# Cross-attention in steps of two batches instead of one, with tails of the context turned on the chip and the last keys loaded once

## The reference, cut to what matters

```python
def cross_attn(x, context, Wq, Wk, Wv):      # x [16,64,512], context [16,1601,512], float32
    Q = x @ Wq
    K, V = (context @ Wk, context @ Wv)
    energy = jnp.einsum('bqd,bkd->bqk', Q, K)
    lengths = jnp.sum(energy[:, 0] != 0, axis=-1)      # counted, then used as a mask
    pad = jnp.arange(Sk)[None, None, :] >= lengths[:, None, None]
    energy = jnp.where(pad, NEG_INF, energy)
    score = jax.nn.softmax(energy / np.sqrt(DK), axis=-1)
    return jnp.einsum('bqk,bkd->bqd', score, V)
```

## Time and profile before

| | us |
|---|---|
| median of 3 runs | 998.28 |
| lowest and highest | 998.18, 999.06 |
| profiled execution | 997.61 |
| its span | 995.7 |

### The profile page before, as it was taken

How to read it: one execution, slowest core, us unless ns; L and a number is a source line. 1 busy time by engine, 2 the same in 40 slices (tenths; PEclk the granted TensorE clock), 3 DMA queues, 4 the chain that set the end, 5 groups by cost and what they waited for, 6 DMA issues and landing times.

```text
span 995.7 us, 14420 instructions
## 1 busy us (share of the span) xinstructions
PE 981.3 (99%) x5412; PEld 775.3 (78%) x5412; DVE 615.6 (62%) x1147; ACT 393.7 (40%) x631; POOL 216.7 (22%) x202
## 2 busy tenths in 40 slices
PE   8999999999999999999999999999999999999998
PEld 4886444445454468878888888999999999999997
DVE  6378543445656566896466668777665665666566
ACT  3332121212111143355667642544444445444441
POOL 2052400002000046454422124631000000000051
PEclk9999999999999999999999999999999999999999
DMA  9709599999999922033311100796674656745543
GB/s 304 313 1 384 243 367 429 432 419 425 428 432 428 404 66 64 3 93 106 111 47 33 32 1 7 270 280 213 181 209 159 188 176 185 187 153 181 163 143 133
DMA packets 47015, 208.97 MB, mean 210 GB/s; under 512 B 5808, under 2 KB 16304, under 8 KB 42736
## 3 DMA queue, kind: packets, MB, share of 16 engines
q1 hardware_dynamic: 41312, 190.02, 52.4%
q0 software_dynamic: 5648, 18.22, 5.4%
HBM read 192.10 MB, written 16.12 MB: 209 GB/s over the span
## 4 chain that ended last, share of the span: by engine, by line
PE 85%; DVE 8%; POOL 2%; issue 2%; DMA 1%; ACT 1%; SPq 1%; POOLq 0%; ACTq 0%; DVEq 0%
PE ps L486 56%; PE ps L650 9%; PE ps L621 8%; POOL xs L2044 2%; DVE stats L1316 2%; PE ps L480 2%; PE ps L631 1%; PE ps L598 1%; PE ps L952 1%; PE ps L654 1%; PE ps L979 1%; PE ps L532 1%; DMA xr<-in_x 1%; DVE hr L1423 1%; PE ps L663 1%
## 5 line engine op out<-in xcount | busy, mean ns | idle before, releaser
L486 PE MATMUL ps<-x,w 128*128 128x320 f32 x1536 | 235.6, 309 | 0.0
L486 PEld LDWEIGHTS ps<-x,w 128*128 128x128 f32 x1536 | 228.0, 188 | 0.4
L1847 DVE TENSOR_TENSOR w<-big,w 128x1536 fp32r<-128x1536 f32 x64 | 112.1, 1753 | 78.3 <-ACT w L1250 78.3
L486 PE MATMUL ps<-hsplit,w 128*128 128x320 f32 x672 | 107.8, 309 | 0.2 <-DVE hsplit L1881 0.2
L1250 ACT CAST w<-big 128x1536 fp32r<-128x1536 f32 x64 | 94.5, 1479 | 29.2 <-PE ps L486 26.8
L486 PEld LDWEIGHTS ps<-hsplit,w 128*128 128x128 f32 x672 | 100.8, 188 | 0.5 <-DVE hsplit L1881 0.4
L621 PE MATMUL ps<-big 128*64 128x512 f32 (+2 forms) x512 | 98.2, 499 | 0.6 <-DVE s_stat L1496 0.6
L486 PE MATMUL ps<-xcT,u 128*128 128x512 f32 x432 | 98.2, 389 | 0.0
L486 PEld LDWEIGHTS ps<-xcT,u 128*128 128x128 f32 x432 | 81.0, 188 | 17.0 <-DVE xcT L1628 0.2
L650 PE MATMUL ps<-big 128*64 128x512 f32 x384 | 86.4, 597 | 0.3
L1272 ACT CAST hsplit<-big 128x320 fp32r<-128x320 f32 x64 | 29.4, 460 | 138.4 <-DVE big L1877 138.4
(11 more groups left out here) (338 smaller groups left out, 1542.6 us busy)
## 6 DMA issues: line engine op xcount, KB each, us to landing
big<-in_ctxT SPq DMA_DIRECT2D x16, 3202.0 KB, 16.9
big<-in_ctx SPq DMA_DIRECT2D x16, 3072.0 KB, 16.8
big<-in_w_units SPq DMA_DIRECT2D x64, 768.0 KB, 4.6
big<-in_dense_units SPq DMA_DIRECT2D x41, 256.0 KB, 2.7
xs<-big POOLq DMA_DIRECT2D x1, 5120.0 KB, 17.6
big<-in_gate_units SPq DMA_DIRECT2D x12, 384.0 KB, 2.9
hr<-xs SPq DMA_DIRECT2D x28, 160.0 KB, 5.8
ys<-big POOLq DMA_DIRECT2D x28, 160.0 KB, 5.5
```

What stands on the lines that cost most here:

```text
L486: mm = nc.tensor.matmul(dst, lhs[x], rhs[w], start=start and x + w == 0, stop=stop and x == 1)
L1847: V.tensor_tensor(wsplit[f % RING][1][:], wraw[f % RING], wsplit[f % RING][0][:].bitcast(F32), ALU.subtract).then_inc(w_low, 1)
```

## The change

The step becomes a pair of batches, p = 0 to 7. The two batches are the two halves of the partitions, each with all 1601 keys, so nothing is split or joined across halves.

- Scores: three pieces of 512 columns for both halves, then the tail of 65 columns in the fourth PSUM bank. VectorE's and ScalarE's passes are over 1601 columns, half as often. The exchange keeps only the count. `clear_pad`, the joining of maxima and sums, and `output_sum` go.
- The tails of a pair come as one tile of 128 rows (64 keys of each batch, `row_tails`). TensorE turns it (`turn_tail`, 4 transposes), ScalarE copies it to `column_tails` (`tail_columns`).
- The last key of all 16 batches is loaded once, as columns and as rows (`end_columns`, `end_rows`). Its probabilities are put in a column of a mask (`end_probability`), turned, and multiplied with `end_rows` (16 rows, all 128 columns). The 64 other tail keys are two products of 64 rows and 64 columns.
- Transposes of probabilities: 12 tiles in three banks, all copied out by ScalarE, and three for the tail.
- The context is loaded in pieces of a pair (4 groups of keys of two batches, 2 MB each) into five ring places and one extra; a load waits for `piece_used`.
- `late_queries` stands in p = 0 to 3 whole. `value_rows` stands in p = 5 to 7, one ahead of the values and one behind; the seventh stands inside the last values.
- SyncE loads the first units of the next stage once 44 pieces are used, and ScalarE takes three of them before the last output copy.

```diff
@@ TensorE
+            def transpose_probabilities(p):
+                pe.wait_ge(exp_done, p + 1)
...
+                for t in range(KT):
+                    if t == 0 and p >= 2:
+                        pe.wait_ge(o_evac, p - 1)
+                    if t == 4:
+                        pe.wait_ge(misc_read, p + 1)
+                        if p:
+                            pe.wait_ge(tail_evac, 3 * p)
+                        if p < PAIRS - 1:
+                            pe.wait_ge(tail_ready, 2 * p + 4)
...
+                    mm = nc.tensor.transpose(ps[:, (7, 0, 1)[t // 4], (t % 4) * P:(t % 4 + 1) * P],
+                                             es[:, t * P:(t + 1) * P], ident[:])
+            def turn_tail(p):
+                pe.wait_ge(row_tail_in[p % 3], x_loads + 16 * (p // 3 + 1))
...
+                for d in range(DC):
+                    mm = nc.tensor.transpose(ps[:, 0 if p else 6, d * P:(d + 1) * P], row_tails[p % 3][:, d * P:(d + 1) * P], ident[:])
+                mm.then_inc(tail_turned, 1)
+            def tail_and_count(p):
+                if p:
+                    pe.wait_ge(pt_evac, 3 * (p - 1) + 2)
+                    nc.tensor.transpose(ps[0:S, 0, 0:P], es[:, KT * P:KT * P + S], ident[:])
+                    nc.tensor.transpose(ps[:, 0, P:2 * P], es[:, KT * P - S:KT * P + S], ident[:])
+                    pe.wait_ge(cnt_done, 2 * p)
+                    mm = nc.tensor.transpose(ps[0:B, 0, 2 * P + 8:3 * P + 8], end_part, ident[:])
+                if p < PAIRS:
+                    pe.wait_ge(cnt_done, 2 * p + 1)
+                    mm = nc.tensor.matmul(ps[:, 0, 2 * P:2 * P + 1], first_rows[:], s_cnt[:, p % 2:p % 2 + 1], start=True, stop=True)
+                mm.then_inc(misc_done, 1)
+            def values(p):
+                for t in range(KT):
...
+                    for half in range(2):
+                        mm = nc.tensor.matmul(ps[half * S:half * S + S, 6, :], pts[:, t, half * S:half * S + S],
+                                              context_at[home(g)][half][:, t % 4, :], start=(t == 0), stop=False)
+                    if t == 3 and p == PAIRS - 1:
+                        value_rows(NT - 2, 3 * PAIRS)
+                pe.wait_ge(tail_evac, 3 * p + 3)
+                for half in range(2):
+                    rows = slice(half * S, half * S + S)
+                    nc.tensor.matmul(ps[rows, 6, :], pts[rows, KT, rows], row_tails[p % 3][rows, :], start=False, stop=False)
+                mm = nc.tensor.matmul(ps[:, 6, :], end_prob[0:B, :], end_rows[0:B, :], start=False, stop=True)
+                mm.then_inc(pv_done, 1)
+            for p in range(PAIRS + 1):
+                if p < PAIRS:
+                    scores(p)
...
+                transpose_probabilities(p - 1)
+                if p >= 2:
+                    transpose_output(p - 2)
+                tail_and_count(p)
+                if p < PAIRS // 2:
+                    late_queries(p)
+                ahead, behind = VALUE.get(p, (None, None))
+                if ahead is not None:
+                    value_rows(ahead, 3 * p)
+                values(p - 1)
+                if behind is not None:
+                    value_rows(behind, 3 * p)
+                if p + 1 < PAIRS:
+                    turn_tail(p + 1)
@@ VectorE
+            def end_probability(p):
+                dve.wait_ge(exp_done, p + 1)
+                if p:
+                    dve.wait_ge(misc_done, p + 1)
+                V.tensor_scalar(end_part, end_mask[:, 14 - 2 * p:30 - 2 * p], es[:, SK - 1:SK], None,
+                                ALU.mult).then_inc(cnt_done, 1)
+            for p in range(PAIRS + 1):
+                if p:
+                    end_probability(p - 1)
+                if p < PAIRS:
+                    count_keys(p)
+                tail_and_count(p)
+                if p < PAIRS:
+                    shift(p)
+                if p:
+                    normaliser(p - 1)
+                if p >= 2:
+                    output_low(p - 2)
+                for i in VALUE.get(p, ()):
+                    if i is not None:
+                        second_norm(i)
...
+                if 4 <= p < 8:
+                    for k in range(ATANH_TERMS - 2 - 2 * (p - 4), max(ATANH_TERMS - 4 - 2 * (p - 4), 0), -1):
+                        decay_term(k)
+                if p == 7:
+                    decay_end()
+                if p == PAIRS:
+                    second_norm(NT - 2)
@@ SyncE
+            def load_piece(rows, p, piece):
+                g = loads[0]
+                loads[0] += 1
+                if g > RINGS:
+                    sp.wait_ge(piece_used, last_in(g) + 1)
...
+            for p in range(2, PAIRS):
+                load_columns(p)
...
+                load_rows_of(p - 1)
+                if p + 1 < PAIRS:
+                    sp.wait_ge(pv_done, p - 1)
+                    load_tail(p + 1)
```

More of the change, by code:

```diff
@@ L38 @@
 FLOOR = -5e37
[L39 to L42, removed]
+VALUE = {5: (0, 1), 6: (2, 3), 7: (4, 5)}
 ATANH_TERMS = 9
+LATE_BANKS = (6, 7, 1, 6)
 def dense_groups():
@@ L398, in _, with load_tail, load_columns, load_rows_of @@
+            def load_tail(p):
+                load(row_tails[p % 3], a["row_tails"][p], row_tail_in[p % 3])
+            def load_columns(p):
+                for piece in range(PIECES):
+                    load_piece(False, p, piece)
+            def load_rows_of(p):
+                for piece in range(PIECES):
+                    load_piece(True, p, piece)
             for i in range(NT):
                 wait_filled(sp, "v", i)
-            load_columns(0)
-            load_context(0)
+            load_piece(False, 0, 0)
@@ L403, in _ @@
+            load_piece(False, 0, 1)
+            load(end_rows[0:B, :], a["end_rows"], consts_in)
+            load(end_columns, a["end_columns"], consts_in)
             for i in range(NT):
                 wait_filled(sp, "z", i)
[L405 to L413, removed]
+            load_tail(0)
@@ L414, in _ @@
+            load_tail(1)
+            loads[0] = 3
+            for piece in range(PIECES):
+                load_piece(False, 1, piece)
+            load_tail(2)
+            for c in range(DC):
+                wait_filled(sp, "m2", c)
+            loads[0] = 2
+            load_piece(False, 0, 2)
+            loads[0] = 2 * PIECES
+            load_rows_of(0)
+            for p in range(2, PAIRS):
+                load_columns(p)
+                if p == 5:
                     sp.wait_ge(late_q, DC)
@@ L610, in scores @@
+            used = [0]
+            def scores(p):
+                if p:
+                    pe.wait_ge(shifted, p)
+                else:
                     for c in range(DC - 1):
                         wait_evacuated(pe, "q", c)
-                for piece, (lo, *widths) in enumerate(PIECES):
-                    if piece and n % 2 == 0:
-                        pe.wait_ge(pad_cleared, n // 2 + 1)
+                if p == PAIRS // 2:
+                    pe.wait_ge(late_q_out, DC)
+                for piece in range(PIECES + 1):
+                    if piece < PIECES:
+                        g = used[0]
+                        used[0] += 1
+                        pe.wait_ge(context_in[home(g)], 16 * fill(g))
+                        columns_in = context_at[home(g)]
+                    else:
+                        pe.wait_ge(tail_ready, 2 * p + 2)
+                        columns_in = column_tails
```

469 lines of the change are left out of this document (202 added, 267 removed).

## The result

| | before | after |
|---|---|---|
| median of 6 runs each, us | 998.15 | 1004.45 |
| lowest and highest | 997.28, 999.06 | 1003.21, 1005.67 |
| profiled execution (its span) | 997.61 (995.7) | 1003.21 (1001.5) |
| start of the first scores | 112.05 | 113.32 |
| start of the last value rows | 362.41 | 368.80 |

The ratio of the medians, after over before, is 1.0065 (95% interval 1.0055 to 1.0075): slower, by 6.3 us. The forecast was 1005.5, in a range from 1001.5 to 1013.

The account below looks back on a forecast made before the run. The prediction took TensorE to bound the kernel, with a transfer some 2 us behind it. Its terms summed to +7.2 us, 1004.8 for the profiled execution and 1005.5 as median, in a range from 1001.5 to 1013.

Parts of the forecast that it names:

- A: Values of each pair: the last key's product takes the whole array for 0.86 us, 8 times; +6.8 us.
- B: Tails of each pair: two 64-row products share two slots, 0.86 us as before; 0 us.
- E: TensorE changes tile shape six times a pair instead of four, two more turns of 0.13 us; +2.1 us.
- Rival 2: Tiles of 64 by 64 don't share a slot (+6.9) or small products cost 0.107 (+5.6): 1011 to 1012.5, both 1018; chance 0.22.
- C: Scores of a pair: a third full piece and 16 small instructions replace two uneven pieces, 4.55 against 4.48 us; +0.6 us.
- D: Transposes and exchange of a pair: fewer instructions, less a small wait for the count, net -0.48 us, 8 times; -3.8 us.
- F: TensorE's idle time shrinks in the first step and goes at n=8 and n=15; -1.5 us.
- G: Last step: the last key's transpose waits for VectorE's end probability, queued behind a second norm and decay; +3.4 us.
- H: End of the stage, last tail product to last value rows: the sum over halves goes, copy and difference grow; -0.4 us.
- Transfers: Context loads through the ring: every piece lands at least 6 us before its use; 0 us.
- rival 1: Transfers pace the cross-attention loop, so fewer bytes make the change faster: 990.2 us; chance 0.08.

Follow-up runs that it names:

- the run with one shape: The kernel after, with half tails and last key zero-padded so that every value product has tiles of 128 by 64: 1002.51 us.
- the two with VectorE's sum: The kernel after with VectorE adding the last key, 128-row half tails and reordered VectorE work: 997.90 us; the same with value rows moved earlier: 996.72 us.
- one shape and the new order: The kernel after with 128 by 64 value tiles, and VectorE's last end probability moved ahead of most of the second norm: 997.29 us, 0.9995 times before.
- score tails twice: The kernel after with the 65-column score piece computed twice for each pair, 16 instructions more: 1008.70 us.
- the repeat: The kernel after, run again with no edit: 1005.02 us, 1.0075 times before.

## Why the prediction was right, and where its steps were not

**What bounds the kernel.** TensorE's written list does, as foretold from the earlier trace rows: a pair without filling work took 26.44 us (26.7 foretold), one with late queries 30.01 (30.1), one with value rows 32.16 (32.3).

**A, B and E: +9.6, foretold 8.9.** The last key and the half tails take 1.05 and 1.01 where the two tails took 0.86. By the run with one shape this splits into 0.86 (A, as foretold), 0 (B: halves of 64 by 64 do lie side by side) and 0.34 for two changes of shape a pair, for which I had 0.26. Rival 2 falls in both its parts. The groups of the last key and of the half tails in the kernel after have nearly the record for an instruction that the earlier trace rows has (592 to 597); by records alone sharing can't be seen, only by the distance of starts:

```profile
L760 PE MATMUL ps<-big 16*128 16x512 f32 x16 | 9.0, 640 | 0.0
L759 PE MATMUL ps<-big 64*64 64x512 f32 x32 | 8.6, 614 | 0.0
```

**C: -3.5, foretold +0.6.** This is the largest miss, a term mis-sized, and it lies far outside the bounds that I gave it (-0.5 to +6.2). Scores of two batches took twice 5.68 us, of a pair 10.92. The 24 full slots are 10.39; the small piece takes 0.53, where I had taken 1.0 and had called 0.86 a lower end. I had built that end from the difference of two records of weight loads (54 ns) in the earlier trace rows; the records overlap for the two halves, and the difference of two records is no slot. Its twin in the kernel before, 2.24 for 577 columns in two unequal halves, I had read rightly.

**D: -2.9, foretold -3.8.** Transposes, count and the turn of a tail take 1.46, 0.52, four of 0.11 to 0.12 and 0.59: 3.02 against 3.38 before. I had counted the twelve and the turn at 0.1145 each, but the turn's four took 0.15 each with their change of shape, and the twelve 0.12.

**F: about -1.1, foretold -1.5.** In the first step TensorE takes 7.81 us from the start of what follows its scores to the next scores (7.4 foretold), 1.3 of it waiting, with the two waits foretold (L724 for the count 0.6, L638 for the last late tile 0.7). The kernel before waited 1.7 there (1.1 and 0.6), not 2.0. The 0.5 each of n=8 and n=15 went: in p=4, which holds what was n=8, nothing is idle any more. A wait of 0.3 for ScalarE's copy (L718, p=1) is new: 1.3 and 0.3, less 1.7 and 1.0, is -1.1.

**G: +3.2, foretold +3.4.** Right in place, cause and size. The chain of the kernel after shows the order of VectorE's list as the forecast walked it, from the second norm through the decay to the end probability:

```profile
347.95 0.75 DVE hr L1424
348.70 0.09 DVE lac L1533
...
349.69 0.25 DVE big L1570
349.94 0.04 issue
349.98 0.28 PE ps L721
```

Not foretold was what follows: in four executions of six the granted clock falls, and the median is 1.2 us above the profiled execution, whose clock didn't.

**H: -0.4, as foretold, in part by luck:** 2.97 us from the end of the last product to the value rows, 3.34 before. The forecast's own figures (3.34, less 0.69, and 0.19 and 0.33 more) make 3.17, not 3.0.

**Transfers: 0, as foretold, for a wrong reason.** No product in the kernel after waits for a transfer. But the slack of 6 us was not there, and the trace of the kernel after shows it. The third piece of the rows of pair 4 (its issue, and its time to landing):

```profile
252.21 0.37 SPq L379 DMA_DIRECT2D big<-in_ctx  x1
...
big<-in_ctx SPq DMA_DIRECT2D x1, 2048.0 KB, 18.8
```

It lands at 271.0, and its first products start at 271.7: 0.7 us to spare. Before it, up to the scores of pair 4, every piece had 6.8 us or more, and the last of the rows of pair 3 still 5.2. In p=4 TensorE needs 26.44 us for a pair and the transfers some 30.3, with 2.5 more for the megabyte of value-row weights asked for there (an estimate from 424 GB/s and the bytes); that is the 6 us. A pair with value rows (32.16 us) gives back 1.9, and the third pieces of rows land 0.7, 2.6 and 4.0 us ahead. The forecast had all of these prices; its walk through the queue isn't on record, so which step of it was wrong can't be said. Three runs agree: the one without the last product and the two with VectorE's sum wait for transfers.

Of rival 1, that bytes pace the loop, it is true that they come next. With one shape and the new order the kernel takes 997.3 and no product waits for a transfer; with less work than that on TensorE (997.9 and 996.7) it does. Rival 1's 990 was out of reach.

**The sum.** 9.6 - 3.5 - 2.9 - 1.1 + 3.2 - 0.4 = +4.9 us. From the first scores to the last value rows the stage grew by 5.1 (255.5 against 250.4), and by 5.6 with the first turn of a tail (L711 at 112.8), which stands ahead of the first scores and is counted in D; so 0.7 is not attributed. The scores start 1.3 us later; less that turn (0.5), 0.7 is a later start. In the profiles of the changed kernels this is anything from 0.1 (score tails twice) to 1.2 us (last key on VectorE), and the kernel before with 65 rows, which has none of these changes, starts its scores 1.4 later; its cause stays open. Behind the stage the kernel after is 0.5 shorter. With the clock (+1.2, less the 0.5 by which the profiled execution of before lay under its median) this makes 6.6 for the 6.3 us of the medians; the rest lies outside the spans. The forecast came out 1 us off because the miss in C (-4.1) was offset by D (+0.9), F (+0.4), E (+0.7), what is not attributed, the later start and the clock. The bound, the direction and G were right by reasoning; that the total came so close is luck, since one term alone was off by four times as much.

## What to carry to other kernels

When the engine that bounds a kernel runs a written list, price each edit by the distance of starts in that list, and look for what is queued ahead of any small operation that it waits for on another engine: one such operation behind a norm cost 3.2 us, and where the clock fell behind the idle time 1.7 us more. Keep one shape of tile through a run of products even where that means zeros in the unused rows; padding was free here and each change of shape was not. Before taking work off the bounding engine, take some away as a trial to learn where the next bound stands: here it was less than 1% below, and a transfer that lands in time says nothing of how near it was until its landing is set beside its use.

## What the runs showed of the hardware that I had not expected

- TensorE's granted clock fell to a mean of 0.58 over 3 us after a wait of 3.2 us in a stage where it had been busy throughout (profile of the repeat); 16 products took 5.28 us for 3.58. Of 28 executions with this wait 22 show a lower mean clock, of 37 without it none. A wait of 0.92 us near the same place left it at 1.00.
- Sixteen float32 instructions of 64 by 65 columns take 0.46 to 0.53 us, 29 to 33 ns each, though the weight load of one has a record of 137 ns.
- A change of tile shape costs 0.15 us (128 by 64 to 64 by 64) and 0.15 to 0.19 (from there to 16 by 128).
- Loading 65 or 80 of 128 partitions for tiles that make up 2% of the bytes lowered the rate of the whole stream from 421 and 426 GB/s to between 396 and 404, with the DMA engines as busy as before.
